# Decoder layer with a routed feed-forward: third normalization split once into two fp16 halves, its transposes moved from TensorE to a transposing DMA of the SP queue

## The reference, cut to what matters

```python
x = x + self_attention(layernorm(x))                 # causal, with a linear bias on the distance
x = x + cross_attention(layernorm(x), ctx_1024)      # 16 heads of 16 features
x = x + ffn(layernorm(x))

def ffn(x):                                          # E = 8 experts, two for each token, F = 1024
    gate_probs = softmax(x @ w_gate)                 # 8 logits for each token
    gate_probs = top2(gate_probs) / its sum
    gu = einsum('bsd,edh->ebsh', x, w_gate_up)       # g, u = halves of gu
    expert_out = einsum('ebsf,efd->ebsd', silu(g) * u, w_down)
    return einsum('bse,ebsd->bsd', gate_probs, expert_out)
```

## Time and profile before

| | before |
|---|---|
| median of 3 runs | 1101.05 us (1100.43 to 1101.15) |
| the profiled execution | 1097.28 us, its span 1095.5 us |
| PE busy, share of the span | 94% |
| DVE, ACT, POOL busy | 59%, 59%, 47% |
| mean granted TensorE clock | 0.987 of full speed |
| attention stage | from 0 to about 486 us |
| one iteration of it | 28.3 us: in the chain that ended last, `DMA q_stack<-q_lo` stands at 207.57, 264.24 and 320.89 us, two iterations apart |
| one expert slot | 8.2 us: SP issues the load of `wgu_sb` at 706.22, 714.42 and 722.62 us |

### The profile page before, as it was taken

One profiled execution on the slowest core, in us unless ns is written; L12 is line 12 of the kernel. 1 busy time (PEld: TensorE's weight loads), 2 busy tenths in 40 slices (PEclk: granted clock), 3 DMA queues, 4 the chain that ended last, 5 costly groups with the idle time before them and its releaser, 6 DMA issues.

```text
span 1095.5 us, 36805 instructions
## 1 busy us (share of the span) xinstructions
PE 1026.1 (94%) x12856; PEld 863.5 (79%) x12856; DVE 648.0 (59%) x2144; ACT 644.5 (59%) x1410; POOL 519.5 (47%) x564
## 2 busy tenths in 40 slices
PE   4689999999999999978989999999999999999994
PEld 2456677767677666646988999999999999999984
DVE  5566777777777787874565444444444444444442
ACT  5678888888888888854443344343343343443431
POOL 4755677777777777523334323223223333223223
PEclk9989999999999999999999999999999999999998
DMA  5654667766666555359122543742635442215761
GB/s 179 208 191 154 179 184 183 183 183 169 174 172 182 168 178 159 100 196 345 41 31 36 150 116 77 248 144 53 199 75 162 135 144 34 34 29 149 299 217 16
DMA packets 92929, 160.84 MB, mean 147 GB/s; under 512 B 21184, under 2 KB 69376, under 8 KB 88000
## 3 DMA queue, kind: packets, MB, share of 16 engines
q1 hardware_dynamic: 77598, 141.83, 40.4%
q0 software_dynamic: 15248, 18.18, 9.8%
q10 hardware_dynamic: 18, 0.01, 0.0%
HBM read 270.75 MB, written 43.07 MB: 286 GB/s over the span
## 4 chain that ended last, share of the span: by engine, by line
PE 81%; DMA 4%; DVE 4%; SPq 4%; ACT 3%; issue 2%; POOL 1%; another core or an unknown queue 0%; ACTq 0%; DVEq 0%; POOLq 0%
PE t_ring L2461 15%; PE front L2461 15%; PE pv L2493 7%; PE s_ring L2493 7%; PE pv L2164 6%; PE s_ring L2131 5%; PE t_ring L2149 4%; PE front L2006 3%; PE front L2015 3%; DMA q_stack<-q_lo 2%; PE front L2064 2%; PE tail L2015 2%; PE s_ring L1993 2%; PE tail L1993 1%; PE tail L2209 1%
## 5 line engine op out<-in xcount | busy, mean ns | idle before, releaser
L881 POOL DMA_INDIRECT out<-y_sb,place_i x64 | 101.8, 1591 | 287.5 <-DVE y_sb L1901 92.7
L1377 DVE TENSOR_REDUCE nmax<-s_ring 128x2 f32<-128x512 f32 x256 | 167.3, 681 | 59.7 <-PE s_ring L2131 57.1
L2461 PE MATMUL t_ring<-rows_hi,wgu_sb 128*128 128x128 f16 x2048 | 193.9, 220 | 1.1 <-issue 1.1
L2461 PE MATMUL front<-rows_hi,wgu_sb 128*128 128x128 f16 x2048 | 192.4, 219 | 1.6 <-DVE rows_lo L1874 1.6
L1048 ACT ACTIVATE probs_t<-t_ring,mask_bias 128x512 f32<-128x512 f32 x256 | 167.1, 701 | 27.4 <-PE t_ring L2149 25.0
L2461 PE MATMUL t_ring<-rows_lo,wgu_sb 128*128 128x128 f16 x1024 | 179.3, 220 | 0.0
L2461 PE MATMUL front<-rows_lo,wgu_sb 128*128 128x128 f16 x1024 | 178.1, 219 | 0.0
L2461 PEld LDWEIGHTS front<-rows_hi,wgu_sb 128*128 128x128 f16 x2048 | 162.7, 98 | 3.9 <-DVE rows_lo L1874 2.1
L2461 PEld LDWEIGHTS t_ring<-rows_hi,wgu_sb 128*128 128x128 f16 x2048 | 163.6, 98 | 2.2 <-issue 0.6
L1238 ACT ACTIVATE silu_g<-t_ring 128x256 f32<-128x256 f32 x136 | 52.3, 384 | 164.0 <-PE t_ring L2461 148.1
L1238 ACT ACTIVATE silu_g<-front 128x256 f32<-128x256 f32 x136 | 52.0, 383 | 161.2 <-PE front L2461 143.9
(11 more groups left out here) (324 smaller groups left out, 2269.1 us busy)
## 6 DMA issues: line engine op xcount, KB each, us to landing
wgu_sb<-gu_split SPq DMA_DIRECT2D x68, 2048.0 KB
wd_sb<-down_split SPq DMA_DIRECT2D x68, 1024.0 KB
w_piece<-in_w_gu SPq DMA_DIRECT2D x32, 512.0 KB
gu_split<-w_halves SPq DMA_DIRECT2D x32, 512.0 KB, 3.8
w_piece<-in_w_down SPq DMA_DIRECT2D x16, 512.0 KB
down_split<-w_halves SPq DMA_DIRECT2D x16, 512.0 KB, 5.1
x_in<-in_x SPq DMA_DIRECT2D x16, 256.0 KB, 3.6
ctx_in<-in_ctx_t_in SPq DMA_DIRECT2D x16, 256.0 KB
```

The lines of the kernel that those rows point to most:

```text
L881: nc.gpsimd.indirect_dma_start(out=out, out_offset=bass.IndirectOffsetOnAxis(ap=place_i[:, j:j + 1], axis=0), in_=y_sb[:, j], in_offset=No ...
L1377: nc.vector.tensor_reduce(nmax[:, n // HJ, :, n % HJ], s_ring[n % 2][:].rearrange("p (r k) -> p r k", r=2), AX.X, ALU.max, negate=True).th ...
L2461: o = nc.tensor.matmul(gu_ring[f][:, part * SLOT:(part + 1) * SLOT], wgu_sb[j][:, w, at:at + P], r[:, j % 2, c], start=(i == 0), stop=(i = ...
```

## The change

The third norm now comes out scaled by 32. `xn3` shares the memory of `o_n`; ACT rounds it to fp16 (`t_xn3`), POOL forms the rest (`xn3_rest`), and both halves lie side by side in `xn3_h`. SP transposes all of a batch in one DMA (`transpose_normed`, 256 KB) into `xn3_t`, from which PE forms the gate logits with six fp16 matmuls for each of the two tiles against a split `w_gate`. The `normed` tensor holds the two halves (the same bytes per row). In the expert stage POOL gathers both halves at once, and SP transposes a slot's rows in one DMA (`transpose_rows`, 128 KB) into `rows_t`; `rows_transposed`, `rows_round` and `rows_rest` are gone. The orders of all engines within an attention iteration are written anew.

```diff
             def store_normed(c, p):
-                sp.wait_ge(ln3_done, c + 1)
-                sp.dma_start(normed[bass.ds(c * S, S)].rearrange("(t p) d -> p t d", p=P), xn3[:, p]
+                sp.wait_ge(xn3_lo, c + 2)
+                sp.dma_start(normed[bass.ds(c * S, S)].rearrange("(t p) d -> p t d", p=P), xn3_h[:, p]
                              ).then_inc(normed_out[p], 16)
+
+            def transpose_normed(c, p):
+
+                sp.wait_ge(xn3_lo, c + 2)
+                sp.sem_inc(sp_passed, 1)
+                sp.wait_ge(gate_ps, c + 1)
+                sp.sem_inc(sp_passed, 1)
+                sp.dma_start_transpose(xn3_t[:].rearrange("p t a n -> p (t a) n"),
+                                       xn3_h[:, p].rearrange("p t d -> p (t d)")).then_inc(xn3t_in, 16)
...
             def iteration(b, p, h, c, t, s, f, n):
+                if c:
+                    transpose_normed(b - 1, 1 - p)
                 if n:
                     load_pieces(b + 3, h + 1 + p, 1 - p)
                 if f and (not isinstance(b, int) or b + 4 < B):
                     load_next(b + 4, p)
+                if s and f:
+                    stack_max(b + 1, 1 - p)
                 if f:
                     store_pieces(b + 2, h + 1, p)
                     stack_rows(b + 2, p)
-                    stack_k_hi(b + 2, p)
-                if s and f:
-                    stack_max(b + 1, 1 - p)
-                if f:
-                    stack_k_lo(b + 2, p)
                     stack_q_hi(b + 2, p)
+                if c:
+                    store_normed(b - 1, 1 - p)
+                if f:
                     stack_q_lo(b + 2, p)
                 if c:
-                    store_normed(b - 1, 1 - p)
                     store_stream(b - 1)
+                if f:
+                    stack_k_hi(b + 2, p)
+                    stack_k_lo(b + 2, p)
...
+            def transpose_rows(j, g):
+                sp.wait_ge(rows_in[j], 16 * g + 16)
+                sp.sem_inc(sp_passed, 1)
+                sp.dma_start_transpose(rows_t[:, j], rows[:, j]).then_inc(rows_t_in[j], 16)
...
             load_down(first, 0)
+            sp.wait_ge(exp_sb, 16 * (B - 1))
+            transpose_rows(0, 0)
+            transpose_rows(1, 0)
             for j in range(1, STREAMS):
...
                     sp.wait_ge(gu_ps, FP * s + FP)
+                    transpose_rows(j, g + 1)
                     load_gate_up(e, j, new)
...
+            def xn3_rest(c, p):
+                pool.wait_ge(xn3_hi, c + 1)
+                nc.gpsimd.tensor_tensor(xn3_h[:, p, :, D:2 * D], xn3[:], xn3_h[:, p, :, 0:D], ALU.subtract
+                                        ).then_inc(xn3_lo, 1)
...
-            def t_xn3t(c):
-                act.wait_ge(xn3t_ps, c + 1)
-                copy(xn3_t[:], as_chunks(tail)).then_inc(xn3t_sb, 1)
+            def t_xn3(c, p, u):
+
+                act.wait_ge(ln3_done, c + 1)
+                act.wait_ge(normed_out[p], 16 * u + 16)
+                act.wait_ge(xn3t_in, 16 * c + 16)
+                act.sem_inc(act_passed, 1)
+                copy(xn3_h[:, p, :, 0:D], xn3[:]).then_inc(xn3_hi, 1)
...
-            def t_xn3t(c, p):
-                pe.wait_ge(ln3_done, c + 1)
-                transpose_tiles(tail, xn3[:, p]).then_inc(xn3t_ps, 1)
-
             def t_gate(c):
-                pe.wait_ge(xn3t_sb, c + 1)
+                pe.wait_ge(xn3t_in, 16 * c + 48)
+                products = [(r, w, k) for r, w in ((HI, HI), (LO, HI), (HI, LO)) for k in range(NC)]
                 for t in range(NT):
-                    for k in range(NC):
-                        o = nc.tensor.matmul(tail[:, t * E:(t + 1) * E], xn3_t[:, k, t * P:(t + 1) * P], wg_sb[:, k],
-                                             start=(k == 0), stop=(k == NC - 1))
+                    for i, (r, w, k) in enumerate(products):
+                        o = nc.tensor.matmul(tail[:, t * E:(t + 1) * E], xn3_t[:, t, NC * r + k], wg_split[:, w, k],
+                                             start=(i == 0), stop=(i == len(products) - 1))
                 o.then_inc(gate_ps, 1)
...
-            def rows_transposed(s, j, g):
-                pe.wait_ge(rows_in[j], 16 * g + 16)
...
-                for c in range(NC):
-                    o = transpose(rows_bank[:, c * P:(c + 1) * P], rows[:, j, c * P:(c + 1) * P])
-                o.then_inc(rt_ps, 1)
...
-                    pe.wait_ge(rlo_sb, s + 1)
+                    pe.wait_ge(rows_t_in[j], 16 * g + 16)
```

More of the change, by code:

```diff
@@ L630, in _, with slot @@
             iteration(15, 1, 7, True, True, False, False, False)
-            store_stream(B - 1)
-            store_normed(B - 1, 1)
-            def slot(s, j, weights, ahead):
+            transpose_rows(2, 0)
+            transpose_rows(3, 0)
+            def slot(s, j, g, weights, ahead):
                 if weights:
@@ L1085, in iteration @@
                     h_exp(b, 0, 1)
+                if f:
+                    f_xnt(b + 2)
+                if t:
+                    h_exp(b, 1, 0)
+                if f:
+                    f_k(b + 2, 1 - p, h + p + 1)
                 if c:
@@ L1135, in iteration @@
                     f_q(b + 2, 1 - p, h + p + 1)
+                if t:
+                    h_out(b, p, 3)
+                if f:
+                    f_v2(b + 2, p)
             def before_last():
@@ L1226, in last_tail, with slot @@
                     t_ont(B - 1)
-                if s == 3 and f == 2:
-                    t_xn3t(B - 1)
-                if s == 4 and f == 1:
+                if s == 3 and f == 0:
+                    t_xn3(B - 1, 1, B // 2 - 1)
+                if s == 4 and f == 3:
                     t_gate(B - 1)
-            def slot(s, j, ahead):
+            def slot(s, j):
                 first = isinstance(s, int) and s == 0
@@ L1241, in slot @@
                         act_round(s, f - 1)
-                    if f == 1 and ahead:
-                        rows_round(s + 1, 1 - j % 2)
                     if f == 2 and j % 2 == 1:
@@ L1593, in iteration @@
                 if s:
+                    h_max(b + 1, 5, 6)
                     h_max(b + 1, 6, 7)
@@ L1938, in slot @@
                         act_rest(s, f - 1)
-                    if f == 1 and ahead:
-                        rows_rest(s + 1, 1 - j % 2)
                     if f == 2 and j % 2 == 0 and not first:
@@ L2237, in iteration @@
                 if f:
-                    f_q1(b + 2)
+                    f_k(b + 2)
+                    f_xnt(b + 2)
+                if t:
+                    h_scores_t(b, p, 1, 0)
+                    h_scores_t(b, p, 1, 1)
+                if f:
+                    f_k_rest(b + 2)
                 if c:
                     t_ont(b - 1)
+                if t:
+                    h_values(b, p, 0)
+                if s:
+                    h_scores(b + 1, q, h + p, 0, 2)
                 if f:
-                    f_k_rest(b + 2)
-                if t:
-                    h_scores_t(b, p, 1, 0)
-                if f:
+                    f_q1(b + 2)
                     f_q1_rest(b + 2)
-                if t:
-                    h_scores_t(b, p, 1, 1)
                 if c:
@@ L2302, in iteration @@
                 if t:
+                    h_scores_t(b, p, 4, 1)
+                    h_values(b, p, 3)
+                    h_scores_t(b, p, 5, 0)
                     h_scores_t(b, p, 5, 1)
+                if s:
+                    h_scores(b + 1, q, h + p, 11, 12)
+                if t:
                     h_values(b, p, 4)
                     h_scores_t(b, p, 6, 0)
+                if f:
+                    f_xn2t(b + 2)
                 if s:
-                    h_scores(b + 1, q, h + p, 11, 12)
-                if c:
-                    t_gate(b - 1)
+                    h_scores(b + 1, q, h + p, 12, 14)
                 if t:
@@ L2312, in iteration @@
                     h_values(b, p, 5)
+                if s:
+                    h_scores(b + 1, q, h + p, 14, 15)
+                if t:
                     h_scores_t(b, p, 7, 0)
+                if c:
+                    t_gate(b - 1)
                 if s:
-                    h_scores(b + 1, q, h + p, 12, 14)
+                    h_scores(b + 1, q, h + p, 15, 16)
+                if f:
+                    f_q(b + 2)
                 if t:
@@ L2525, in slot @@
                         last_tail(s, f)
-                    if ahead and f == 1:
-                        rows_transposed(s + 1, (j + 1) % STREAMS, g + (j + 1) // STREAMS)
                     if f >= 2:
```

337 lines of the change are left out of this document (148 added, 189 removed).

## The result

The changed kernel takes 1237.53 us (median of 4 runs, 1235.01 to 1238.31) against 1100.74 us (1099.24 to 1101.15) for the kernel before on the same chip: a ratio of 1.1237, 95% interval 1.1215 to 1.1259. It is slower by one eighth. The forecast was 1223 us, slower, by rival A.

The account below looks back on a forecast made before the run. PE bounds the expert stage; attention has two near-equal limits, PE's work and a loop through SP's queue. 92 + 24 + 21 - 15 = +122 on the profiled 1097.3 us gives 1219, about 1223 against 1101; range 1120 to 1315.

Parts of the forecast that it names:

- rival A: Main case, the sum of all terms: 1223 us, own range 1165 to 1260; chance 0.55.
- SP's chain, +92: Attention iterations: SP's issues from `h_max` to the next `h_scores` take 15.8 us, PE waits 8.4; +92 us over 14.
- about -1.0 for the small waits of PE: Attention iteration: PE's small waits vanish in the long one, about -1.0 us each iteration, between 0 and 1.5.
- The clock, +24: Attention iterations: PE's clock dips behind each 8 us pause, losing 1.7 us, 14 times: +24 us, bounds 0 and 48.
- The transposing DMA in an iteration: Attention gate: 4.4 us are left for issue and landing of 256 KB; 3.6 us taken for landing, so no stall.
- The passage, +21: Attention to experts: gates of batches 14 and 13 wait for transposing DMAs behind weight loads, +16 and up to 5 us.
- Experts, -15: Expert stage: two fp32 transposes, 0.22 us, leave PE in each of 68 slots, -15 us.
- The gate's matmuls: Attention gate: twelve added fp16 matmuls of 8 columns per batch, 0.6 us taken, bounds nothing and 1.3 us.
- Rival B: rival A with a 10.4 us transposing DMA stalling the gate 6 us in 14 iterations, +84: 1307 us; chance 0.14.
- E: SP limits the expert stage, 12 us per slot, +243 on top of rival A: 1466 us; chance 0.06.
- C: Attention: PE's work decides, SP's chain fits into 7.4 us with issues of 0.1 us: 1075 us, faster; chance 0.12.
- D: Attention: SP's chain partly hidden, half the stall, no clock dip, +32: 1133 us; chance 0.10.

Follow-up runs that it names:

- run 1: The kernel before with only SP's statements of an attention iteration put in the changed kernel's order: 1232.19 us, ratio 1.1233.
- run 6: The changed kernel with 60 constant matmuls added on PE ahead of its wait for `k_lo` in each iteration: 1230.89 us, ratio 1.1182.
- Run 2: The changed kernel with SP's iteration put back in the order of before, the transposing DMA still first: 1231.48 us, ratio 1.1219.
- run 8: All new operations, with every engine's iteration in the order of before and SP's last iteration behind stream 1's loads: 1105.7 us, ratio 1.0047.
- run 7: The changed kernel with SP's last attention iteration moved from behind stream 3's weight loads to behind stream 1's: 1216.44 us, ratio 1.1088.
- run 10: The changed kernel with gate and up weight loads issued ahead of the transposing DMA in each expert slot: 1233.48 us, ratio 1.1255.
- run 4: Run 2's kernel with GpSimd's third weight-piece subtraction moved ahead of that of the third feature-major normalisation: 1193.69 us, ratio 1.0856.
- run 11: Run 9's kernel with one ScalarE exponential moved ahead of the third weight piece, and PE's gate later: 1123.52 us, ratio 1.0233.
- run 9: Run 8's kernel with transposing DMAs, loads, SP's last iteration and batch 13's gate reordered to cover waits for transposing DMAs: 1099.56 us, ratio 1.0020.

## Why the prediction was right, and where its steps were not

The marks of the two profiled executions put the 137.7 us (1233.2 less 1095.5) in their places. The gate of batch 13 starts 126.9 us later (605.35 against 478.43), 3.5 of it its own wait; between it and the gate of batch 14 another 20.4 us go (46.1 us against 25.7); from there to the end 9.6 us come back (581.7 against 591.35).

- **SP's chain, +92.** The mechanism was right and is shown by run 1. Its length was forecast at 15.8 us and is 15.55. The wait was forecast at 8.4 us and is 7.3 (102.0 us in the 14; a wait of 1.55 us precedes them), since PE has 8.1 us to do beside the chain and not 7.4.
- **The part beside the chain.** Forecast as 28.3 + 6.7 less 15.8, or 19.2 us, and 1.7 more for the clock; it is 21.9. The term "about -1.0 for the small waits of PE" failed: in PE's new order there are new ones, about 1 us per iteration for the exponentials (15.1 us in 38 waits).
- **The clock, +24.** The dip came, 0.50 for 6 us, 4 of them with work for PE. The step "behind it PE is the limit" failed: with the dip removed, run 6 gives back some 6 us, and 0.25 us in the iteration read. The term stands in the sum for waits that I had not counted. Chain and clock together were forecast at +116. Up to the gate of batch 13, its own wait aside, 123.4 us are lost; with the 5.0 us that the start gives back, the iterations cost about +128.
- **SP's chain as the only cause.** This stood behind the sum unsaid, and it failed. Run 2 takes the long chain away and gains nothing. GpSimd's late subtraction of the weight piece reaches SP's queue within 0.4 us of the maxima, and the cycle over it is as long. I had priced `xn3_rest` as 1.17 us on an engine "with time to spare" and had not asked what is queued behind it.
- **The transposing DMA in an iteration.** No stall, as taken, and the 3.6 us taken for the landing hold up where no load was issued just ahead. The one such landing that the chain of after shows comes 3.11 us after the issue (602.19). In the iterations of after the gate starts 5.2 to 5.7 us behind the issue and never waits. In run 8, where two loads of 256 KB are issued just ahead of it, the same DMA takes up to 5.45 us, and four gates wait for it. The Trainium skill has two rules on this. "Advanced Engine Details and Errata", X-Bar Transpose (TRN2), has transposing DMAs as fast as plain ones: with 3.11 us against 3.6 for a plain load of 256 KB the trace agrees. "VectorE: DVE Perf Modes", The three transpose paths, gives 1309 ns for one block (its row is of bf16, not fp16); the estimate of 10.5 us that the prediction made of it, eight blocks one behind the other, is not borne out.
- **The passage, +21.** It is 3.5 and 20.4 us. The landing depends on the loads issued ahead, which run 7 shows.
- **Experts, -15.** A slot is 0.22 us shorter, as forecast, and 68 make 15.0; but only 9.6 us come back. The waits of 3.3 and 1.2 us near the end take most of the rest. Their cause is open (run 10).
- **The gate's matmuls** took 0.31 us instead of the 0.6 taken.
- **The start.** The forecast has no term for it; it gives back 5.0 us.

The near number, 1223 against 1237, is thus a right main term and some luck: the clock term stood in for other waits, and the iterations (12 us more than forecast), the passage (3 more) and the experts (5 less given back) are in part hidden by the 5 us at the start. Rival B fell with gates that do not wait in the iterations, E with issues of 1.22 us in the slots, C and D with the waits of 7.3 us. In run 4 the shorter cycle over GpSimd still sets an iteration of 34.3 us. What each of the new orders of PE, DVE and ACT costs, between run 4 with the passage mended (some 1178 us, by 16 us less) and run 8, no run separates.

## What to carry to other kernels

Where a cycle of engines is nearly as long as the work of the fullest one, draw the whole cycle and every way into it: a queue that issues in order starts with the latest of its inputs, and undoing one late input shows nothing while a second is as late. Test the cause both ways: the suspect alone in the old kernel tells whether it suffices, the suspect undone in the new one whether it is the only one. Before an instruction is moved forward, ask what the one in its place was waiting beside.

## What the runs showed that I had not expected

A transposing DMA holds the issuing engine much longer behind queued loads: its issue takes 1.31 us (median of 16), 2.79 us behind one stream's loads (run 7) and 16.26 us behind three streams' loads, where the plain load right ahead of it took 0.33 us. It also moves small pieces: the change brings the packets from 92929 to 146817, and the DMA engines' share in the expert stage from 0.45 to 0.60, without slowing a slot. And a TensorE at half clock for 4 us of its work cost 0.25 us in the iteration read, where other engines were the limit (run 6); in run 11, where they were not, a dip of the same depth behind a wait of 1.9 us goes with iterations 1.4 us longer than those of run 9.
